# First block of a Mamba-2 + ternary FFN kernel: weights land in places used later, x_proj is split by columns, B, C and dt are projected tile by tile, POOL makes part of the high halves

## What is computed

```
xn = layernorm(x)                                  # x: 2 sequences x 2048 x 512
xz = xn @ in_proj_w.T                              # 512 -> 2 x 1024: branch and z half
branch = silu(causal_conv4(branch) + conv_b)
proj = branch @ x_proj_w.T                         # 1024 -> 1024 (X), 16 (dt), 128 (B), 128 (C)
dt = softplus(dt @ dt_proj_w.T + dt_proj_b);  A = -exp(A_log) * dt
Y = ssd(X * dt, A, B, C) + X * D                   # state-space scan over the sequence
attn = (Y * silu(z)) @ out_proj_w.T
q(w) = clip(round(w / (mean|w| + eps)), -1, 1)     # ternary weights w1, w2, w3
ffn = (sigmoid(xn @ q(w1).T) * (xn @ q(w2).T)) @ q(w3).T
out = x + attn + ffn
```

## Time and profile before

| | us |
|---|---|
| median of 3 runs | 1708.71 |
| lowest and highest | 1708.35, 1709.79 |
| the profiled execution's own time | 1710.45 |
| its span, first to last instruction | 1708.6 |
| busy in it: TensorE / VectorE / ScalarE / POOL | 1636.8 / 1018.5 / 843.5 / 455.0 |

### The profile page before, as it was taken

One profiled execution on the slowest core, in us unless ns is written; L12 is line 12 of the kernel. 1 busy time (PEld: TensorE's weight loads), 2 busy tenths in 40 slices (PEclk: granted clock), 3 DMA queues, 4 the chain that ended last, 5 costly groups with the idle time before them and its releaser, 6 DMA issues.

```text
span 1708.6 us, 25097 instructions
## 1 busy us (share of the span) xinstructions
PE 1636.8 (96%) x9490; PEld 806.4 (47%) x9490; DVE 1018.5 (60%) x1674; ACT 843.5 (49%) x1742; POOL 455.0 (27%) x465
## 2 busy tenths in 40 slices
PE   6487889999999999999999999999999999999999
PEld 3243434544445444454445454454544544445444
DVE  6756776566556654655555665556656565566552
ACT  5675535455264543554344552545436554356431
POOL 3323212133032330333212331313403232033320
PEclk9698989999999999999999999999999999999999
DMA  6354330111001110011101110011100111002100
GB/s 220 107 155 147 105 113 17 45 60 40 26 11 53 62 50 1 26 57 44 50 1 39 56 56 25 7 57 50 41 22 13 64 49 50 1 26 69 51 6 25
DMA packets 47080, 89.68 MB, mean 52 GB/s; under 512 B 5968, under 2 KB 6736, under 8 KB 46960
## 3 DMA queue, kind: packets, MB, share of 16 engines
q1 hardware_dynamic: 46960, 88.08, 16.2%
HBM read 79.41 MB, written 8.65 MB: 52 GB/s over the span
## 4 chain that ended last, share of the span: by engine, by line
PE 89%; DVE 5%; ACT 2%; issue 2%; DMA 1%; POOL 0%; SPq 0%; DVEq 0%; ACTq 0%; POOLq 0%
PE bank L544 18%; PE bank L462 17%; PE bank L526 9%; PE bank L560 9%; PE bank L395 9%; PE bank L379 8%; PE bank L405 5%; PE bank L501 3%; PE bank L478 3%; PE bank L493 2%; PE bank L516 2%; PE bank L418 1%; ACT edc L752 1%; PE bank L365 1%; DVE wx_lo L975 1%
## 5 line engine op out<-in xcount | busy, mean ns | idle before, releaser
L462 PE MATMUL bank<-wx_hi,arena 128*128 128x512 f16 x1024 | 317.7, 380 | 0.0
L544 PE MATMUL bank<-xt_hi,q 128*128 128x512 f16 x704 | 267.1, 379 | 0.0
L544 PE MATMUL bank<-xt_lo,q 128*128 128x512 f16 x704 | 267.1, 379 | 0.0
L1296 POOL TENSOR_TENSOR xs<-xs,dsk 128x512 f32<-128x512 f32 x64 | 66.8, 1043 | 645.0 <-DVE xdt L1030 645.0
L462 PE MATMUL bank<-wx_lo,arena 128*128 128x512 f16 x512 | 194.8, 380 | 0.0
L1043 DVE TENSOR_TENSOR edc<-edc,gt 128x512 f32<-128x512 f32 x128 | 90.5, 748 | 125.4 <-ACT edc L757 125.4
L560 PE MATMUL bank<-q,arena 128*128 128x512 fp8e4 x704 | 162.4, 379 | 0.0
L462 PEld LDWEIGHTS bank<-wx_hi,arena 128*128 128x128 f16 x1024 | 100.8, 98 | 127.7 <-issue 16.2
L752 ACT ACTIVATE edc<-csl,csv 128x128 f32<-128x128 f32 x512 | 155.8, 390 | 0.0
L1101 DVE SCALAR_TENSOR_TENSOR full<-tnh,bank 128x512 f32<-128x512 f32 x88 | 60.5, 687 | 115.3 <-PE bank L544 114.1
L782 ACT CAST arena<-full 128x512 f16<-128x512 f32 x88 | 54.6, 620 | 136.3 <-DVE full L1101 136.3
(11 more groups left out here) (170 smaller groups left out, 3248.5 us busy)
## 6 DMA issues: line engine op xcount, KB each, us to landing
csl<-sums SPq DMA_DIRECT2D x128, 256.0 KB, 3.2
res<-w_ffn SPq DMA_DIRECT2D x41, 256.0 KB, 3.6
res<-x SPq DMA_DIRECT2D x32, 256.0 KB, 3.9
out<-res SPq DMA_DIRECT2D x32, 256.0 KB, 2.0
arena<-w_x SPq DMA_DIRECT2D x8, 640.0 KB, 4.7
yac<-x SPq DMA_DIRECT2D x16, 256.0 KB, 2.6
gate<-x SPq DMA_DIRECT2D x16, 256.0 KB, 3.6
arena<-w_in SPq DMA_DIRECT2D x8, 512.0 KB, 7.0
```

The source lines that it names most:

```text
L462: i = pe.matmul(banks[0][:], act[:, k, c * P:(c + 1) * P], wt[:, k, hf * half:(hf + 1) * half], start=(n == 1), stop=(n == 3 * ki))
L544: i = pe.matmul(banks[2 * (m % 2) + j][:], q12[:, j, k, m * P:(m + 1) * P], part[:, k, :], start=(n == 1), stop=(n == 2 * kd))
L1296: pool.tensor_tensor(by_head(xs[u % 2][:], hd), by_head(xs[u % 2][:], hd), heads_over(dsk[:], hf * hph, hph, hd), ALU.mult).then_inc(S["sk ...
```

## The change

- Transfers and stage: x is loaded ahead of the identity. The four branch pieces of `w_in` land in four places of `arena` (`win_stage`), the four z pieces in `wo` (`z_stage`), with no ring and no wait. `w_x` is split by columns: B and C's 256 columns of all k-tiles come as one transfer into `q12` (`bc_stage`); X's 1024 columns as 16 pieces 128x512 (`wx`, new first entries of `prep`), through a ring of eight (four `res`, two places in `q3`, two `yt`).
- Engines: z's high parts are made by POOL (`z_hi`: two before tile 0, two after tiles 0 and 1) instead of ScalarE. POOL's memsets stand ahead of `root`. VectorE scales the taps in `root`. The parts of `w_in` and of xt alternate, and TensorE starts branch tile 0 k-tile by k-tile. `s_hi`/`s_lo` of tile m - 2 are made within tile m, B and C's parts within tiles 4 and 5.
- Projections: in block 0 `project_first` takes dt, B and C k-tile by k-tile into six banks as each `s_lo` is done, after `acc` of tile 7. The softplus reads dt from four banks. `project_x` waits for its `wx_lo`.
- Preparation: the three places before unit 0 get 0, 8 and 8 `wx` pieces instead of 4, 4 and 4 `mag`. SyncE issues the last eight behind the sums. All of `mag`, `wout`, `tern` moves back: units get 12, 12, 12, 7, 6, 6, 6, 7 entries instead of 12, 12, 6, 6, 5, 5, 5, 5. The first four loads go to `full[0]`, `full[1]`, `res[1]`, `res[3]` (`early_ring`). The product that sums the magnitudes uses bank 3 instead of 7.

```diff
-BESIDE_PROJ = [4, 4, 4]
-BESIDE_UNIT = [[3, 3, 3, 3], [3, 3, 3, 3], [2, 2, 1, 1], [1, 2, 2, 1],
-               [2, 1, 1, 1], [2, 1, 1, 1], [2, 1, 1, 1], [2, 1, 1, 1]]
+BESIDE_PROJ = [0, 8, 8]
+BESIDE_UNIT = [[3, 3, 3, 3], [3, 3, 3, 3], [3, 3, 3, 3], [2, 2, 2, 1],
+               [2, 1, 2, 1], [2, 1, 2, 1], [2, 1, 2, 1], [2, 2, 2, 1]]
...
-    prep = [("mag", n) for n in range(12)] + [("wout", k) for k in range(ki)]
+    prep = [("wx", n) for n in range(halves * ki)]
+    prep += [("mag", n) for n in range(12)] + [("wout", k) for k in range(ki)]
...
             def load_prep(kind, n):
-                if kind == "mag" or kind == "wout":
+                if kind == "wx":
+                    s, _ = slot(8, n)
+                    if n >= 8:
+                        sp.wait_ge(S["wx_lo"], n - 7)
+                    hf, k = divmod(n, ki)
+                    sp.dma_start(wx_ring[s], w_x[k * P:(k + 1) * P, hf * half:(hf + 1) * half]).then_inc(
+                        D[f"wx_in{s}"], DMA)
+                elif kind == "mag" or kind == "wout":
                     use = early.index((kind, n))
                     s, _ = slot(4, use)
-                    if use >= 4:
+                    if use < 2:
+                        sp.wait_ge(S["w2_mm"], 1)
+                    elif use < 4:
+                        sp.wait_ge(S["wx_lo"], 8 + 2 * use - 3 + 1)
+                    else:
...
-                for _ in BESIDE_PROJ:
-                    aside()
+                aside()
+                aside()
                 sums_out(b)
                 sums_in(b, 0)
+                aside()
...
+            def project_first():
+                pe.wait_ge(S["acc"], at(0, "acc", 7))
+                for k in range(ki):
+                    pe.wait_ge(S["s_lo"], at(0, "s_lo", k))
+                    for c in range(chunks):
+                        for n, (act, wt) in enumerate(passes(s_parts, w2)):
+                            i = pe.matmul(banks[dt_banks[c]][:, c * heads:(c + 1) * heads],
+                                          act[:, k, c * P:(c + 1) * P], wt[:, k, :],
+                                          start=(k == n == 0), stop=(k == ki - 1 and n == 2))
+                    if k == ki - 1:
+                        i.then_inc(S["dt_mm"], 1)
+                    if k == 0:
+                        pe.wait_ge(S["bc_lo"], 2)
+                    for bk, col, name in ((banks[3], di, "b_mm"), (banks[4], di + ns, "c_mm")):
+                        for n, (wt, act) in enumerate(passes(wx, s_parts)):
+                            i = pe.matmul(bk[:], wt[:, k, col:col + ns], act[:, k, :],
+                                          start=(k == n == 0), stop=(k == ki - 1 and n == 2))
+                        if k == ki - 1:
+                            i.then_inc(S[name], 1)
...
-            for n in range(kd):
-                k, cols = win_pieces[n]
-                stage_hi(n, win[0][:, k, cols], di)
-            turned(0)
-            for n in range(kd, 2 * kd):
-                k, cols = win_pieces[n]
-                stage_hi(n, win[0][:, k, cols], di)
+            win_hi(0)
+            turned(0, (0, 1))
+            win_hi(1)
+            turned(0, (2, 3))
+            win_hi(2)
+            win_hi(3)
             act.wait_ge(D["taps_in"], 3 * DMA)
             act.wait_ge(S["taps_scaled"], 3)
-            for m in range(ki + 1):
+            for m in range(ki + 2):
                 if m < ki:
                     x_branch(0, m)
-                    stage_hi(2 * kd + m, wx[0][:, m, :], width)
-                if m:
+                if m in (4, 5):
+                    bc_hi(m - 4)
+                if 1 <= m <= ki:
                     silu(0, m - 1)
...
+                if m >= 2:
+                    s_hi(0, m - 2)
...
         def gpsimd_program(pool):
+            def z_hi(k):
+                pool.wait_ge(D[f"z_in{k}"], DMA)
+                pool.tensor_scalar(win[0][:, k, di:2 * di], z_stage[k], W_SCALE, None,
+                                   ALU.mult).then_inc(S["z_hi"], 1)
...
             pool.memset(ones[:], 1.0).then_inc(S["cleared"], 1)
+            root(0)
+            z_hi(0)
+            z_hi(1)
             for m in range(ki):
                 x_branch(0, m)
+                if m < 2:
+                    z_hi(2 + m)
```

More of the change, by code:

```diff
@@ L105, in mamba_ffn_block @@
               *(f"x_in{n}" for n in range(4)), *(f"res_in{n}" for n in range(4)),
-              *(f"stored{n}" for n in range(4)), *(f"stage{n}" for n in range(4)),
+              *(f"stored{n}" for n in range(4)), *(f"win_in{n}" for n in range(4)),
+              *(f"z_in{n}" for n in range(4)), "bc_in", *(f"wx_in{n}" for n in range(8)),
               *(f"early{n}" for n in range(4)), *(f"late{n}" for n in range(3)),
@@ L148, in mamba_ffn_block @@
         hid = arena[:].rearrange("p (k q t) -> p k q t", k=kf, q=2)
-        stage = [arena[:, 2 * n * width:2 * (n + 1) * width].bitcast(F32) for n in range(4)]
+        win_stage = [arena[:, 2 * k * di:2 * (k + 1) * di].bitcast(F32) for k in range(kd)]
+        z_stage = [wo[k // 2][:].rearrange("p k n -> p (k n)")[:, 2 * (k % 2) * di:2 * (k % 2 + 1) * di]
+                   .bitcast(F32) for k in range(kd)]
+        bc_stage = q12[:].rearrange("p j k n -> p (j k n)")[:, 0:8 * ki * ns].bitcast(F32).rearrange(
+            "p (k n) -> p k n", k=ki)
+        wx_later = [q3[:].rearrange("p k n -> p (k n)")[:, 4 * n * half:4 * (n + 1) * half].bitcast(F32)
+                    for n in range(2)]
         gt = sb("gt", [P, chunks, P])
@@ L290, in store @@
                 sp.dma_start(rows(out, c, b), res[c][:]).then_inc(D[f"stored{c}"], DMA)
-            sp.dma_start(idn[:], ident).then_inc(D["ident_in"], DMA)
             for c in range(chunks):
                 load_x(0, c)
+            sp.dma_start(idn[:], ident).then_inc(D["ident_in"], DMA)
             for dst, src in ((cw, conv_w), (cb, conv_b), (wdt, w_dt)):
                 sp.dma_start(dst[:], src).then_inc(D["taps_in"], DMA)
[L297 to L304, removed]
+            for k in range(kd):
+                sp.dma_start(win_stage[k], w_in[k * P:(k + 1) * P, 0:di]).then_inc(D[f"win_in{k}"], DMA)
+            for k in range(kd):
+                sp.dma_start(z_stage[k], w_in[k * P:(k + 1) * P, di:2 * di]).then_inc(D[f"z_in{k}"], DMA)
+            for n in range(halves):
+                sp.dma_start(full[n][0:heads, :], w_xdt[:, n * half:(n + 1) * half]).then_inc(
+                    D["small_in"], DMA)
+            sp.dma_start(upp[:], upper).then_inc(D["small_in"], DMA)
             for dst, src in ((dtb, dt_bias), (na, a_log), (dsk, d_skip)):
@@ L307, in sync_program @@
                     D["small_in"], DMA)
[L308 to L314, removed]
+            sp.dma_start(bc_stage, w_x[:, bc].rearrange("(k p) n -> p k n", p=P)).then_inc(D["bc_in"], DMA)
             for b in range(nb):
@@ L370, in x_branch @@
                 bk = banks[4 + m % 4]
-                if m == 0:
+                if m == 0 and b:
                     pe.wait_ge(S["xt_lo"], at(b, "xt_lo", 3))
@@ L455, in project_x @@
                     pe.wait_ge(S["out_ready"], at(b - 1, "out_ready", 0))
+                if b == 0 and u < halves:
+                    pe.wait_ge(S["wx_lo"], (u + 1) * ki)
                 n = 0
@@ L655, in scalar_program, with turned @@
         def scalar_program(act):
-            def turned(b):
-                for k in range(kd):
+            def turned(b, ks=range(kd)):
+                for k in ks:
                     act.wait_ge(S["x_turned"], at(b, "x_turned", k))
@@ L849, in aside @@
                             before[0] = (kind, n)
-                if b == 0:
-                    for m in range(ki):
-                        s_hi(0, m)
                 project_z(b, 0)
@@ L1144, in prep_second @@
             def prep_second(kind, n):
-                if kind == "wout":
+                if kind == "wx":
+                    hf, k = divmod(n, ki)
+                    cols = slice(hf * half, (hf + 1) * half)
+                    part(wx[1][:, k, cols], wx_ring[n % 8], wx[0][:, k, cols], "wx", n)
+                elif kind == "wout":
                     dve.wait_ge(S["wout_hi"], n + 1)
-                    dve.scalar_tensor_tensor(out=wo[1][:, n, :], in0=res[early.index((kind, n)) % 4][:],
+                    dve.scalar_tensor_tensor(out=wo[1][:, n, :], in0=early_ring[early.index((kind, n)) % 4][:],
                                              scalar=W_SCALE, in1=wo[0][:, n, :], op0=ALU.mult,
@@ L1192, in aside @@
                             before[0] = (kind, n)
-                if b == 0:
-                    for m in range(ki):
-                        s_lo(0, m)
                 aside()
```

161 lines of the change are left out of this document (102 added, 59 removed).

## The result

| | before | after |
|---|---|---|
| median, us | 1708.95 (four runs, 1708.35 to 1709.79) | 1720.94 (four runs, 1718.90 to 1722.09) |
| ratio, 95% interval | 1 | 1.0069 (1.0051 to 1.0086) |
| the profiled execution's own time / span | 1710.45 / 1708.6 | 1718.9 / 1717.1 |
| d0 / d1 / F | 89.8 / 99.45 / 228.56 | 88.74 / 99.49 / 235.88 |
| first 16 products of the FFN from F (chain) | 3.86 | 5.00 |

The change makes the kernel 0.7% slower. In the profiled executions the spans differ by 8.5 us. Nothing of it lies ahead of d1, 7.3 lie between d1 and F, and 1.1 in the first 16 FFN products, where TensorE's clock comes back later; from there on both kernels take the same time.

The account below looks back on a forecast made before the run. Ahead of the first FFN product TensorE was not the bound; chains of ScalarE, VectorE and transfers ruled. Front 0 plus units 8.7, less one, gave 1718.2 for the profiled execution, 1716.5 as median; range 1704.5 to 1723.

Parts of the forecast that it names:

- d0: Point where ScalarE starts unit 0's decays; forecast at 88 us, against 89.8 in the kernel before.
- d1: Point where ScalarE starts unit 1's decays; forecast at 99.5 us as before, gain 0.
- F: First FFN product of block 0, from which TensorE is busy without a gap; forecast near 236 us, 228.5 before.
- The likeliest case: Whole kernel: no gain by unit 1's decays, 8.7 us lost from there to the first FFN product; chance 0.52.
- the bounds: Front gain at unit 1's decays put at 0, between -3 and +7; one microsecond was taken off the sum for this.
- the third rival: Front: z's high parts on POOL take 2.5 us each and hold VectorE, +4, so 1720.5; chance 0.12.
- POOL's high parts: Front, z half of w_in: each 128x1024 part takes 1.5 us on POOL, bounds 0.9 and 2.5.
- The exclusion of POOL and VectorE: Front: VectorE's two-input low parts wait out POOL's work; two high parts before 20 delay them by up to 3 us.
- Idle TensorE and the clock: Front: TensorE idles 11 us from near 43 to 54, then runs at clock 0.5, costing dt 2.6 us.
- The moved weights: Before unit 0's decays: eight w_x pieces issued behind the sums cut the gain from 8.0 to 1.8 us.
- The units: From unit 1's decays to the first FFN product: twelve moved pieces make it 137.8 instead of 129.1 us, +8.7.
- The rival on the other side: Faster: early start outweighs moved pieces, 1707, or 1704 with C not behind the transfers; chance 0.15.

Follow-up runs that it names:

- e4: The changed kernel with z's four high parts made by ScalarE instead of POOL: 1715.58 us, 5.4 below the changed kernel.
- e1: The changed kernel without the first 12 magnitude pieces, its units loaded as in the kernel before: 1711.79 us, 9.1 below the changed kernel.
- e6: The changed kernel with one ternary piece moved from the last unit to the one before: 1719.16 us, ratio 1.0066 to the kernel before.
- e3: The changed kernel with all sixteen w_x pieces loaded ahead of the running sums (8, 8, 0): 1713.28 us, 7.7 below the changed kernel.
- e5: The changed kernel with z's high parts on ScalarE, w_x pieces 9 and 7 ahead of the sums, one ternary piece from unit 7 to 6: 1704.47 us.

## Why the prediction was right, and where it was off

The time was forecast as 1716.5, in 1704.5 to 1723, slower most likely; it is 1720.9. The likeliest case (nothing gained at d1, 7 to 9 us lost in the units) is what the profile shows: forecast +7.8 on the span, found +8.5. That the two sums come so close is in part luck: the units cost 1.4 less than the 8.7 forecast, 1.0 was taken off for the bounds, and 1.1 at F was not in the sum. In front of d1, too, two errors cancel in this profile, as the first point below says. And the median lies nearer to the third rival (1720.5, with POOL's parts at 2.5 us each) than to the forecast: POOL's parts were as dear as that rival had them. Step by step:

| step | predicted | after |
|---|---|---|
| rstd scaled / normalising ends | 11.3 | 8.13, 0.17 us / 10.2 |
| tile 0 read | 22 | 19.80 |
| one z high part on POOL | 1.5 (0.9 to 2.5) | 2.76 |
| tile 7's bank free | 54 | 52.9 |
| dt complete | 68.4 | 66.7 |
| softplus ends | 73.8 | 71.96 |
| sums out | 75.5 | 74.65 |
| C made | 87.1 | 87.64 to 88.2 |
| d0, d1 | 88, 99.5 | 88.74, 99.49 |
| stages to F | 20.7, 21.9, 18.3, 16.7, 19.4, 19.1, 21.7 | 19.0, 21.0, 19.0, 15.5, 19.7, 19.1, 23.0 |
| d1 to F | +8.7 | +7.3 |

- **POOL's high parts: the term was mis-sized.** I took 1.5 because one input lay nearer the memset; it is 2.76, above even the upper bound of 2.5, which was twice the two-input add. The bound was unsound: it scaled the width and took the kind of instruction for granted. The third rival priced them at 2.5 (+4), and e4 puts the whole of POOL's part against ScalarE's at 5.4 us. Trainium skill, "GPSIMD Engine Reference", Performance versus the Vector engine, would have given 2.3 as an estimate, nearer than mine, though the instruction measured there is an add of two inputs. In the profile of after the error doesn't show at d1, because tile 0 was ready 2.2 us earlier than I had put it: normalising ended 1.1 earlier, and the exclusion, charged with 1.8 ahead of tile 0, cost one low part 0.8. In the profiles of e1 and e6 it does, where d1 is 1.4 and 2.8 later than forecast.
- **The exclusion of POOL and VectorE** was right in the main: 2.06 us for a low part that takes 1.22 elsewhere. Trainium skill, "SBUF — State Buffer", Who interferes with whom: a VectorE instruction with two SBUF inputs and a POOL instruction that reads SBUF shut each other out for a whole instruction. The rows agree that the two hold each other up (0.84 us more for the low part at 17.86, and 6.33 for POOL's pair where the two later ones take 5.5 together); that it is always for a whole instruction they don't show, for the two low parts at 15.59 take 2.35 us, full speed, while POOL's high parts are on record as running.
- **Idle TensorE and the clock** were right. TensorE waits 10.2 us, to 52.95, and its first k-tiles of B and C run slow. The chain of waits shows the first and the third:

```profile
53.43 2.57 PE bank L464 x6
...
58.70 1.31 PE bank L464 x6
```

  2.57 us for six products at the slower of the two clocks, 1.31 at full clock; the second six, between these, take 2.10. I had 2.6 us for the whole loss; from the chain it is (2.57 - 1.31) + (2.10 - 1.31) and 0.2 for dt: 2.3.
- **The moved weights** were right, mechanism and size: the gain that the sums had was to shrink from 8 to 1.8 us at d0, it shrank from 8.7 to 1.1. e3 confirms it by taking the wait away, and e5 by leaving only 2.15 us of it.
- **The units** were right in sum, and off in single stages by up to 1.7 (by its own terms, 18.4 + 0.9 + 0.2, the fifth stage should read 19.5). The heavy ones came out shorter (19.0 and 21.0 for 20.7 and 21.9), which I put down to the stalls that the earlier trace rows holds and that I carried over with it; no run shows that. The last came out longer: F's wait is 3.5 where I had 2. Divided by the nine more magnitudes and three more of `w_out`, the 7.3 us are 0.6 each, the same as ScalarE's 620 ns of the earlier trace rows. By the stage rows ScalarE is busy for 7.7 us more from d1 to F (84.4 against 76.7) and VectorE for 1.0 more, so that a piece costs what it keeps ScalarE busy is the likely reading. It is argued, not shown: ScalarE's waits for loads grew as well, from 9.6 to 12.8 us, and no run kept the loads and left out only ScalarE's pass.
- **Not in the sum: the clock at F.** The 16 products from F take 5.00 instead of 3.86 us (3.45 for the 16 behind them, at full clock). With 7.3 this makes the 8.5 of the spans. The clock is at half in both kernels some us ahead of F; what differs is when it comes back. Busy tables of before (two rows), after (two), e5 and e6, with the granted clock as the third number from the end:

```profile
222.00:228.56 6.56, 4.26 (x31) 2.77 (x32) 6.13 (x10) 2.26 (x4) 2.80 (x3) 0.50 0.30 82
229.40:230.00 0.60, 0.60 (x5) 0.29 (x3) 0.60 (x2) 0.60 (x1) 0.00 (x0) 1.00 0.95 355
...
232.50:234.50 2.00, 0.00 (x0) 0.00 (x0) 1.32 (x4) 0.64 (x2) 0.00 (x0) 1.00 0.69 179
235.88:238.20 2.32, 2.32 (x6) 0.89 (x7) 2.29 (x5) 0.35 (x1) 0.00 (x0) 0.50 0.49 184
...
222.14:228.00 5.86, 5.86 (x14) 2.04 (x15) 3.48 (x7) 1.75 (x3) 0.00 (x0) 0.50 0.32 93
...
237.42:241.05 3.63, 3.63 (x18) 1.78 (x19) 3.50 (x7) 0.63 (x1) 0.00 (x0) 1.00 0.38 130
```

  In before it is at half up to F and back within 0.9 us. In after it had come back by 232.5, when TensorE had just begun its wait of 3.5 us, fell again in that wait, and was at half for the first 2.3 us of the FFN. In e5 it stays at half for 5.9 us behind F; in e6 it is back ahead of F. Over the nine profiles these products take 3.63 (e1, e6), 3.86 (before), 4.04, 4.50, 4.92, 5.00, 5.31 and 6.58 us (e5): up to 3 us hang on when the clock comes back, and no step of mine had this.
- **Not in the sum: the median.** I carried the difference of two spans over to the median of before. The medians lie 3.5 us further apart than the profiled executions. 2.0 to 2.3 us of that are shown as a possible difference: the profiles of e1, e3 and e6, whose front up to tile 7 is that of after (e1 has one more memset), take up the first z piece 2 us later than the profile of after and keep this to tile 7. That the other executions of after fell so too is likely from this, but argued; no trace shows them.
- **The rival on the other side.** It was to decide once d1 lies before 92, and to end at 1704 if C isn't behind the transfers. Its condition was not met in the change, since POOL's parts didn't fit into VectorE's waits. e5 met it by other means, with d1 at 85.7, and took 1704.5. That the two times agree is luck: the rival had a smaller gain at d1 and 5 to 6 us for the pieces, where e5 has 7.3, and 2.7 in the products from F.

## What to carry to other kernels

Work moved out of waits isn't free where it lands: twelve pieces that cost nothing in waits of ScalarE cost 9 us in a stretch where ScalarE is in the chain. As a first price of a moved piece, take its duration on the engine that ends the stage there. When a chain is shortened by nine us, look at what the next instruction of that engine waits for: here transfers issued behind the shortened step, and eight of them moved ahead gave 7.7 us back. Work given to POOL was paid three times here: the instruction was 2.6 times as long as on ScalarE, it held VectorE up, and it delayed POOL's own share of the next tile.

## What the runs showed of the hardware

- A POOL multiplication by a constant, 128x1024 from f32 to f16, takes 2.76 us (with VectorE's taps beside it, a pair of which takes 2.23 to 2.31 us there and 1.53 in later tiles); ScalarE does it in 1.06 and VectorE's low part of the same piece, with two inputs, in 1.22. POOL's two-input add over 128x512 takes 1.26, that is 2.5 ns per element of a partition against 2.7: one input fewer, with a conversion to f16 that the add doesn't have, made nothing cheaper per element there.
- The front that runs through POOL passed a late start on: where the first z piece is taken up 2.07 us later (16.31 against 14.24), tile 7 is read 2.28 later (53.91 against 51.63). With these parts on ScalarE two profiles agree to 0.04 us, but both take up the first piece at 16.5, so whether that order would absorb a late start isn't shown.
- TensorE's clock at the start of the FFN differs from one profile to the next by up to 3 us of time (3.63 to 6.58 for 16 products), with the wait just ahead no guide to it: e5 waits 1.53 us and pays most, e6 waits 1.93 and pays next to nothing (3.45 is the time at full clock). It goes with the granted clock at F, which is at half for 5.9 us in e5 and full in e6.
